# Delta rule in joined TensorE turns: the output product beside the next chunk's product, u and w in one turn, with the order redrawn

## The reference, cut to what matters

```python
u = T @ v_c
wm = T @ kb_c                 # T: inverse of a unit triangular 32x32 matrix

def step(S, xs):              # one chunk of 32 tokens
    q_i, k_i, u_i, w_i, wm_i = xs
    u_i = (u_i - wm_i @ S) * w_i[..., None]
    a = jnp.where(causal, q_i @ jnp.swapaxes(k_i, -1, -2), 0.0)
    o_i = q_i @ S + a @ u_i
    return (S + jnp.swapaxes(k_i, -1, -2) @ u_i, o_i)

o = o_l + o_g                 # both gate sets
```

## Time and profile before

| | us |
|---|---|
| median of 3 runs | 1227.69 |
| lowest, highest | 1219.04, 1230.57 |
| the profiled execution | 1230.62 |
| its span | 1229.3 |

### The profile page before, as it was taken

One profiled execution on the slowest core, in us unless ns is written; L12 is line 12 of the kernel. 1 busy time (PEld: TensorE's weight loads), 2 busy tenths in 40 slices (PEclk: granted clock), 3 DMA queues, 4 the chain that ended last, 5 costly groups with the idle time before them and its releaser, 6 DMA issues.

```text
span 1229.3 us, 30949 instructions
## 1 busy us (share of the span) xinstructions
PE 1153.7 (94%) x11842; PEld 918.7 (75%) x11842; DVE 906.9 (74%) x1894; ACT 704.4 (57%) x2020; POOL 837.9 (68%) x1156
## 2 busy tenths in 40 slices
PE   5887879999989999999999999999999999999998
PEld 3454558887768878777887887887778977788886
DVE  4947888986788868975587688987678766764544
ACT  5787787566756564466654666456776433332222
POOL 3745378688688745699579728699659837874870
PEclk9888889999999999999999999999999999999999
DMA  7101085765546575864478447785346867886763
GB/s 263 35 24 50 6 268 181 215 193 173 168 139 194 201 224 172 259 215 152 137 235 258 147 164 254 221 264 171 124 120 225 263 193 249 249 283 211 263 235 106
DMA packets 91186, 230.67 MB, mean 188 GB/s; under 512 B 9888, under 2 KB 16160, under 8 KB 90912
## 3 DMA queue, kind: packets, MB, share of 16 engines
q1 hardware_dynamic: 90896, 228.11, 57.8%
q10 hardware_dynamic: 144, 0.59, 0.1%
HBM read 225.51 MB, written 3.15 MB: 186 GB/s over the span
## 4 chain that ended last, share of the span: by engine, by line
PE 28%; DVE 12%; DMA 5%; POOL 4%; ACT 4%; issue 3%; SPq 1%; DVEq 0%; POOLq 0%; ACTq 0%
PE bank L896 8%; PE bank L943 6%; DVE ogate L1351 2%; PE bank L824 2%; POOL vgate L1737 2%; DMA kv<-values 2%; PE bank L933 2%; PE bank L914 2%; DMA vgate<-gates 2%; PE bank L610 1%; PE bank L924 1%; DVE kv L1120 1%; PE bank L907 1%; PE bank L669 1%; DMA gates<-xn 1%
## 5 line engine op out<-in xcount | busy, mean ns | idle before, releaser
L1737 POOL TENSOR_TENSOR vgate<-vgate,xT 128x512 f32<-128x512 f32 x256 | 324.9, 1293 | 68.7 <-DMA vgate<-gates 68.6
L896 PE MATMUL bank<-wv,vgate 128*128 128x128 f32 x2048 | 253.0, 278 | 0.6 <-POOL vgate L1737 0.4
L896 PEld LDWEIGHTS bank<-wv,vgate 128*128 128x128 f32 x2048 | 244.4, 193 | 9.6 <-issue 4.5
L943 PE MATMUL bank<-ogate,wo 128*128 128x256 f32 x1024 | 243.1, 383 | 1.7 <-DVE ogate L1351 1.4
L943 PEld LDWEIGHTS bank<-ogate,wo 128*128 128x128 f32 x1024 | 188.3, 190 | 31.8 <-issue 6.8
L1351 DVE TENSOR_TENSOR ogate<-ogate,bank 128x1024 f32<-128x1024 f32 x128 | 152.2, 1213 | 25.7 <-PE bank L933 19.1
L1621 ACT ACTIVATE mprob<-bank,mmin 128x256 f32<-128x256 f32 x128 | 59.3, 469 | 122.2 <-DVE mmin L1340 122.1
L1462 ACT ACTIVATE prob<-prob,mx 128x128 f32<-128x128 f32 (+1 forms) x256 | 96.0, 377 | 37.8 <-DVE mx L1056 37.4
L1669 POOL TENSOR_TENSOR rot<-rot 128x512 f32<-128x512 f32 x64 | 81.5, 1273 | 44.6 <-DVE rot L1032 44.5
L610 PE MATMUL bank<-wqkv,hT 128*128 128x512 f32 x192 | 107.0, 664 | 2.5 <-ACT hT L1398 1.4
L1714 POOL TENSOR_TENSOR dlt<-dlt,step 128x126 f32<-128x126 f32 (+22 forms) x248 | 92.8, 374 | 19.4
(11 more groups left out here) (224 smaller groups left out, 2354.2 us busy)
## 6 DMA issues: line engine op xcount, KB each, us to landing
ogate<-gates SPq DMA_DIRECT2D x128, 512.0 KB, 4.5
vgate<-gates SPq DMA_DIRECT2D x128, 512.0 KB, 4.4
wo<-in_wo_moe SPq DMA_DIRECT2D x128, 256.0 KB, 4.9
wv<-in_wv_moe SPq DMA_DIRECT2D x128, 256.0 KB, 4.8
kv<-values SPq DMA_DIRECT2D x64, 256.0 KB, 5.4
local<-in_local SPq DMA_DIRECT2D x1, 1715.0 KB, 9.5
wqkv<-in_wqkv SPq DMA_DIRECT2D x2, 768.0 KB, 6.4
x<-in_x SPq DMA_DIRECT2D x8, 128.0 KB, 5.0
```

Of the source, the lines that this page charges most:

```text
L896: i = nc.tensor.matmul(out[:, n * D:(n + 1) * D], xg[:, e, n * P:(n + 1) * P], m.wv[slot][:, e, :], start=(q, n, e) == (0, 0, 0), stop=(q, ...
L943: i = nc.tensor.matmul(out[:, 0:T], m.wo[slot][:, e, :], cg[:, e, :], start=(h, q, e) == (0, 0, 0), stop=(h, q, e) == (MH - 1, 1, EQ - 1))
L1737: i = tt(gate[:, e:e + half, :], gate[:, e:e + half, :], spread(m.xT[b % 2][:, :], 1, half), ALU.mult)
```

## The change

`uw` of both halves is one turn on TensorE and one on VectorE, with two banks instead of one. `du` of chunk c issues, behind its own products, those of `dout` for chunk c-1; only the last chunk's `dout` keeps a turn of its own. The bank of the outputs is taken ahead of `du` of chunk 1. The delta stream no longer has empty ticks between its stages, the strings of letters and the banks are drawn anew; no product, vector operation or DMA is added or removed, and all sizes stay. TensorE has 1250 turns in place of 1314, VectorE 1281 in place of 1289; the other engines' counts stay.

```diff
 def delta_ticks(b):
     ticks = [[("kk", b)], [("dstart", b)], [("w0", b)], [("lanes", b)]] + [[("sub", b, part)] for part in range(len(SUBS))]
-    ticks += [[("dT", b)], [("uw", b, 0)], [("uw", b, 1)], [("st0", b)]]
+    ticks += [[("dT", b)], [("uw", b)], [("st0", b)]]
     for c in range(NC_):
-        ticks += [[("du", b, c)] + ([("dout", b, c - 1)] if c else []), []]
-        if c < NC_ - 1:
-            ticks += [[("ds", b, c)], []]
+        ticks += [[("du", b, c)]] + ([[("ds", b, c)]] if c < NC_ - 1 else [])
     return ticks + [[("dout", b, NC_ - 1)], [("dres", b)], [("drms", b)], [("dwo", b)]]
...
-KEPT = [("gla_sum", "gsum", (0,)), ("delta_sum", "dout", (0,)), ("moe_sum", "mproj", (0, 0)), ("values", "hv", (0,)),
+KEPT = [("gla_sum", "gsum", (0,)), ("delta_sum", "du", (1,)), ("moe_sum", "mproj", (0, 0)), ("values", "hv", (0,)),
...
-         "fT": 1, "fsel": 1, "din": 2, "l2": 1, "dgate": 1, "kk": 1, "uw": 1, "du": 1, "ds": 1,
+         "fT": 1, "fsel": 1, "din": 2, "l2": 1, "dgate": 1, "kk": 1, "uw": 2, "du": 1, "ds": 1,
...
 (TensorE)
-    def uw(b, a):
-        bank = banks.of("uw", b, a)
-        out = split(take(bank), n=NC_)
-        pe.wait_ge(s.vkc, nth("dstart", b))
-        pe.wait_ge(s.winvT, nth("dT", b))
-        for c in range(NC_):
-            i = per_head(out[:, c, :], m.winvT[:, a * NC_ + c, :], flat(m.vkC[:, c, :, :]), start=True, stop=True)
-        i.then_inc(bank.filled, 1)
+    def uw(b):
+        for a in range(2):
+            bank = banks.of("uw", b, i=a)
+            out = split(take(bank), n=NC_)
+            pe.wait_ge(s.vkc, nth("dstart", b))
+            pe.wait_ge(s.winvT, nth("dT", b))
+            for c in range(NC_):
+                i = per_head(out[:, c, :], m.winvT[:, a * NC_ + c, :], flat(m.vkC[:, c, :, :]), start=True, stop=True)
+            i.then_inc(bank.filled, 1)
 
     def du(b, c):
+        if c == 1:
+            take(banks.kept("delta_sum", b))
         bank = banks.of("du", b, c)
...
         i.then_inc(bank.filled, 1)
+        if c:
+            dout(b, c - 1)
 
     def dout(b, c):
         bank = banks.kept("delta_sum", b)
-        out = take(bank)[:, c * CH:(c + 1) * CH]
+        out = bank.ap[:, c * CH:(c + 1) * CH]
...
 (VectorE)
-    def uw(b, half):
-        bank = banks.of("uw", b, half)
+    def uw(b):
         v.wait_ge(s.dw, nth("dgates", b))
-        rows = m.uw[:, half * NC_:(half + 1) * NC_, :, :].rearrange("p c a t -> p c (a t)")
-        tt(rows, chunks(filled(bank)), spread(m.gates[b % 2][:, 2 + half, :], 2, 2 * CH), ALU.mult).then_inc(bank.emptied, 1)
+        for half in range(2):
+            bank = banks.of("uw", b, i=half)
+            rows = m.uw[:, half * NC_:(half + 1) * NC_, :, :].rearrange("p c a t -> p c (a t)")
+            tt(rows, chunks(filled(bank)), spread(m.gates[b % 2][:, 2 + half, :], 2, 2 * CH), ALU.mult).then_inc(bank.emptied, 1)
...
 TENSOR_TURNS = (
     "GaaaaGGGaaaaaXabbabbaGbbbabaabGbbabacaaacbGbGGaccabGcbbaaabbGbGGbaabGbaababbcabacbbbcbcbbGGcbbabaaccGaaaaacbbc"
-    "GGabaczbCaCbaaGAabFACGGGGaaAbbaaababbabbbcVaVaVaFAAaAcbVPVcAPcAAcAbbVzbaPaAaaCbbPFbCGbGVbVbbAAbcAaaPbacVbbVbAc"
+    "GaGbaczbCaCbaaAaGbAFCGGGGaaAbbaaababbabbbcVaVaVaaAAFcAbVPVcAPcAAcAbbVzbaPaAaCabCbPFbGGVbbVbbAAbcAaaPbacVVbbbAc"
...
```

More of the change, by code:

```diff
@@ L88 @@
[L88 to L92, removed]
@@ new lines @@
+    "DbaCDAaFCAPVVFAaDGAbbPbAEDbAbVbVCbPAbPbAVAcAVcPFAPAcAVAVPcAPGGaAcVAVAPPaAaaAVAVAPPaaAFAAVAVaaabbGPAPFDAAbGAGVV"
+    "aPaGPbbbbDaDAaDbbDaDAbDbADbacaDaDcbaDADbDPDaDcbDaGGDGaVcADDcbbbbaVbabaAAbGPbaEabAcPcPAVcAAcAVPaacbbzAaAAPAaVPP"
+    "CabCAbbVbVAAbbAPPDAVbVbAACVAPFbPbAVAAcVAPcDGVADPAcGDADVADPDVDAVDAFADPVGDAcVVDADPDADcDFVADGGVAVGVDDPAVEGPPzAAAP"
+    "CCPAFAAAPPAAAVCAVVPAPAVAPDVADVDPDADFDADAFDADPDPDADVDADAVDADPDPAVAADDAPPVAEVAAVAPPAAAVAPPAVAAVAPPAVAAAPPAVADAPA"
+    "DPDVDADVDADAVDADPDPDADVDADAVDADPDPAADPPE")
@@ new lines @@
+VECTOR_TURNS = (
+    "VaaaaaaaGaaaaabGGGGbbaGbbGGbGbaabGGGaaGGGGacaGcbacabbGbccccbGaabbGaabaabGaabbcGGGcGbbcGGbbGGbccccGGGaaGcaaGcGG"
+    "caaGbaaabbccccGzCCabbCCCCCCCCGbaaAFAGaaFFaabGFaaabGGbabbcGGbGGVaaVOOcFAaAVcaGVGcccOOAcbAVzCVbCaabaabFCCCFGFVVG"
+    "bOGbbcACCbAOcGcGGbVCbVCbGCbOVVODDAGADFcccFOOFVcVAcFAcacOaOVAVAaaGOOcccAcAaaDOGODaAbAaDbbGFDDbVVbDGbaaDGGDaDaGG"
+    "bDGGDObGGDODAVVDaADaDaDaGGDGGFGFcFbVDcbbcGbVDGDAbAGVVDEbDbDbOOcccaGacOzCOCAaAGaVVaaCCCCCOOAFAVFFCVCOOFaaAVVCAa"
+    "aDFDOODAAVVGcbDcbbDcGbODFGDGGFAOcDccAFGGcGzbCObDOGCGbDCCADCDbAVVCCDCDODOCDcCDADcVAVcDFDFDFcVccVGDFDGEDOOcGGFAa"
+    "VGAaVGGGFaOOAaFAaaVVFOOaaAAbaaOObbDAbADDVVaOOaAaaAVbVbaabaDaDbVVDGDDbcDbbDOcbOcDAVAVcccDcDGbDDbDbDODObAVDAVGDD"
+    "GaaDDGaDcGOGcOcAVGAaGVGEGGaaOOVVAAGGGGcccGGOGGAOAcaaazCbCVOVODbDDACCACGbVGOObaAVbACGCCVVCDbCaaOOaDAabAFDFbFVOV"
+    "ODFADAcDDcDcDaaODOccDcbDaDcabbzDCbCDVVDDAFCCDACCCCVCbEFOVbbFACAbOFDDVGaVGGDOOcAGGVAcGVGGcGFOOAVFAFaVcccOOFcGGV"
+    "VGAGAGGGGaaOOaaAVVAaaOOFAVVAbaabbDFbFGOOADADVVFbDGDbbDaDabDODaDaOcDaDacDbDcaDbbDaADbDGDADDcccDDcbDbbaabVVOaaOE"
+    "GAacaAGGcGcGGGOOGGcAccVAVcbzaaObbOAbCACCCbVVCbCCOOADbACCbVVCOOVVDADAFFFOOFcVVAAcDcDGGDOODGGDAVVGDAGGGDVDVOODFD"
+    "AAVcccVDDDODcDFOFDVFVGDADGADDDEGzCVOVCAOACCCCVOOVACACCCOOAFAVVFFODOVVFDDADADDDDVDODOADFFAVDFFDDDODOVDVADADDDOO"
+    "DDAADVVEOOVVAAOOAAVVOOAAVVOOAADOODDADADVDVDDODOVDVADADDDDODOVDADADDDOOE")
@@ L136 @@
+    "voovoovvoovoovoovoooE")
 BANK_TURNS = (
[L137 to L140 removed]
@@ L150 @@
+    "43756365627143521432514325143271721503714023570437504372543743032574305743507243707243254242530743027503247057"
+    "45450402546520456205642054025025042765423615426054126072160267015640721504710574605410675401740561472016473250"
+    "46172056142756041276104726507467052476054265407")
 PACKS = {
```

76 lines of the change are left out of this document (30 added, 46 removed).

## The result

The changed kernel took **1234.56 us** (median of 16 runs, 1226.08 to 1242.48), the kernel before 1225.51 beside it (16 runs, 1219.04 to 1230.82): ratio 1.0079, 95% interval 1.0060 to 1.0099. It is 9 us slower, where 1226 us (a gain of 1.8 us) had been forecast. In two later comparisons the same kernel stood at 1.0058 (1.0033 to 1.0084) and 1.0067 (1.0041 to 1.0093). The profiled execution took 1239.8 us against 1230.6.

A forecast was written before the change was run, and what follows sets the result against it. TensorE's work plus its 75.6 us of idle time, 43.3 in play, was taken to bound the kernel; -1.2 - 1.3 - 0.8 - 2.5 + 4.0 = -1.8 us gave 1226 us, range 1211 to 1240.

The forecast's parts named there:

- `uw` in one turn: Delta rule on TensorE: both halves together 1.92 us, 0.14 us less for each of six pairs; -0.8 us.
- one long wait (over 3 us): Stated sign of being wrong: small moves of the strings shift a DMA or VectorE operation so that such a wait appears.
- Output joined to `du`: Delta rule on TensorE: ten moved outputs each save 0.12 us by standing directly behind the next `du`; -1.2 us.
- Fewer changes of size: TensorE: groups of 32x32 products between larger ones fall from 151 to 144, 0.19 us each; -1.3 us.
- The wait on GpSimd in sequence 6, the seventh: Joined output's 1.64 us wait on `dlt_sum` and the half clock behind it mostly go; 0 to 3.2 gained, -2.5 us taken.
- Tighter hand-overs: Products handed over between engines and PSUM banks retaken stand closer, so TensorE waits more; +4.0 us, ends -10 and +11.
- The first 134 us: Start of the program, before the orders first differ on TensorE: out of reach, equal within a microsecond.
- GpSimd did not hold the joined turn: Rival: joined `du` waits while GpSimd is inside its gates, 3.2 us a place, five places; 1242 us, chance 0.12.
- the first rival: GpSimd's gates hold the joined `du` and everything behind it, 3.2 us a place; slower, 1242 us, chance 0.12.
- Banks did not bind: Rival: two banks held at once by `uw`, bank waits triple from 5 to 15 us; 1234 us, chance 0.13.
- The second rival: New order frees half of TensorE's 43.3 us idle time in play; about -20 us, hence 1208 us, chance 0.18.
- "same" by 1%: Whole kernel neither faster than 1215.4 us nor slower than 1240 us; chance 0.65.

The follow-up runs named there:

- 40 waits: Changed kernel with 40 more wait instructions on TensorE in an idle stretch near 30 us: 1226.57 us (1.0033), in a second comparison 1230.05 us (1.0038).
- the one cut comparison: Changed kernel with vgate, wv and wo transfers cut to a quarter plus 40 hidden waits, 1219.13 us; kernel before with the same cut, 1223.05 us.

## Why the prediction was wrong, step by step

**The step that failed** is the `uw` in one turn, priced at -0.8 us. Its own time was right (301.71 to 303.63, 1.92 us). What it did to TensorE's supply of instructions was left out, a term put at nothing: in the profiled execution 10.0 us of stall, in two later ones of the same kernel 3.9 and 8.1, in the kernel before none, with half clock behind some of them. The text had named "one long wait (over 3 us)" as what would make it wrong; there were three, but I looked for a DMA or VectorE as the cause. The old order did have two such pairs, adjacent and without a stall, and I took them as proof that the burst is free. One was at the edge of a stall (0.04 us by the line).

**Output joined to `du`** (-1.2): a joined turn takes 0.39 us to the next (1117.24 to 1117.63), as forecast. The part alone measured 0.9997, with an interval (0.9974 to 1.0020) too wide to show 1.2 us.

**Fewer changes of size** (-1.3): not separable. Without stalls TensorE's busy time in the changed kernel was 1145.9 us (40 waits), below the 1151 to 1153 forecast, and 1157.5 with them, so the clock moves it more than overlap does.

**The wait on GpSimd in sequence 6, the seventh** (-2.5): gone, no `dlt_sum` among the waits, as forecast. The clock was to stay up there. It fell, behind the stall at 1102.4 to 1105.7 us, and with 40 waits it was 1.00 to the end: the term was right where the stall did not take its place.

**Tighter hand-overs** (+4.0): wrong in sign. Other idle time fell by 4.6 us in the profiled execution, of which 1.6 is the wait on GpSimd that has a term of its own; idle time from 134 us on is 48.5 us, 38.5 without the three stalls, and 36.4 in all with 40 waits, against 43 to 47 forecast. The count of hand-overs under a threshold did not predict waiting. The term's own sum was off too: half of 3.4 is 1.7 us, not 2.3, which would have made it +3.4.

**The first 134 us** were equal, as said: 101.54 against 101.67 us busy.

**The rivals.** GpSimd did not hold the joined turn (no wait on `dlt_sum`); the first rival gave the right sign for a wrong reason. Banks did not bind in the changed kernel's profile; that this rival's 1234 us is what was measured is luck. The second rival, an order that frees waits, may have been partly right and hidden: 3.9 us in the one cut comparison, not 18 (and half of its 43.3 would be 21.7). Its measure, the busy share of the weight loads, was 75% before and after and shows nothing of the stalls. The measured 1234.6 lay in the range (1211 to 1240), and "same" by 1% had held most of the chance; but no case in it had this mechanism, so that is luck as well. Not settled is also what exactly a fetch waits behind: less data shortened the delays, but the number of transfers under way at the request hardly told a short delay from a long one (median 2.6 us with none, 3.4 with 14 or more). Nor is it settled how much of the extra half clock the stalls cause; two of the changed kernel's stretches at 1.2 GHz follow other waits (2.06 us on `vloc`, 2.62 on `qkT`), and the stall at 978 us has none behind it.

## What to carry to other kernels

Joining turns of many tiny matmuls makes a burst of instructions, and instructions are a supply like any other: look for idle time released by "issue" in the middle of a turn, and count the records in the burst before pricing a join. Where such a stall shows, shift the program by a few dozen cheap instructions in an idle stretch, and see whether the stalls change while the order stays: 40 waits gave back 5 of the 10 us between the medians of one comparison here. One profile is not enough to judge by, since the same kernel had 10.0, 8.1 and 3.9 us of stalls in three. An adjacent pair without a stall in one profile is not proof that the burst is free, since the margin may be hundredths of a microsecond.

## What the runs showed of the hardware

TensorE's instructions came in packets of 16,384 bytes, one for 256 records (95 packets; 103 with 2,048 more records), through their own DMA queue. From the earliest place of request TensorE had 288 records in hand; the packet took 1.0 us, and 1.2 to 1.5 us passed from its end to the start of the next matmul where TensorE had stalled. The start was delayed by 1.1 us at best, 3.1 in the middle and up to 12.5, less with less data moving (median 2.2 at 130 MB). A satisfied wait cost TensorE some 50 ns (96, 192 and 256 of them).

The Trainium skill (Runtime: NRT & Kernel Launch, Instruction fetch mechanics) says that the instructions are refilled in 16 KiB blocks of 256 by the sequencer's own DMA queue; the packets and their count agree. It calls the cost of crossing a block's edge "mostly hidden"; here 31 stalls of 1 us and more stood at such edges, up to 4.06 us, and 22.5 us in one kernel. It also gives TensorE room for 2,048 instructions; the 288 in hand at the earliest request show no such reserve.
